# A retention layer and a quantized FFN on one core: the recurrence in halves of 64 tokens, one mask operation on VectorE, and an order written out call by call

## The reference

```python
q, k = rope(x @ Wq), rope(x @ Wk)          # 8 heads of 16 columns
v, g = x @ Wv, x @ Wg                      # 8 heads of 32 columns
s = log2(1.0 - exp2(-5.0 - arange(8)))
decay = where(diff >= 0, exp2(diff[None] * s[:, None, None]), 0.0)   # diff = query - key position
scores = einsum('bhqd,bhkd,hqk->bhqk', q * 16 ** -0.5, k, decay)
o = einsum('bhqk,bhkd->bhqd', scores, v)
o = o * rsqrt(mean(o * o, axis=-1) + EPS) * g_norm_w
x = layernorm(x + (o * (g * sigmoid(g))) @ Wo)
h = silu(fp4_linear(x, w_gate)) * fp4_linear(x, w_up)   # fp4_linear quantizes both operands
x = layernorm(x + fp4_linear(h, w_down))
```

## Time and profile before

| | us |
|---|---|
| median of 3 runs (137.73 to 137.95) | 137.76 |
| span of the profiled execution | 135.8 |
| PE busy | 121.6 (90%) |
| DVE busy | 112.9 (83%) |
| ACT busy | 98.0 (72%) |
| POOL busy | 96.6 (71%) |

### The profile page before, as it was taken

How to read it: one execution, slowest core, us unless ns; L and a number is a source line. 1 busy time by engine, 2 the same in 40 slices (tenths; PEclk the granted TensorE clock), 3 DMA queues, 4 the chain that set the end, 5 groups by cost and what they waited for, 6 DMA issues and landing times.

```text
span 135.8 us, 3550 instructions
## 1 busy us (share of the span) xinstructions
PE 121.6 (90%) x1248; PEld 79.6 (59%) x1248; DVE 112.9 (83%) x391; ACT 98.0 (72%) x311; POOL 96.6 (71%) x139
## 2 busy tenths in 40 slices
PE   4997998999999999999999999999999958888660
PEld 4755574755656566575758584848484745445450
DVE  1269889876879899999999999999999899999710
ACT  3055665778858787787888888888888978876753
POOL 4212856878677778878787979797979697656561
PEclk9999999999999999999999999999999999999999
DMA  3899980000000000000000000000000000000011
GB/s 105 262 250 237 409 288 5 7 2 0 5 0 0 5 0 2 0 7 0 0 5 0 0 7 19 0 19 7 19 0 24 0 19 19 22 19 19 27 54 59
DMA packets 6897, 6.53 MB, mean 48 GB/s; under 512 B 864, under 2 KB 6112, under 8 KB 6752
## 3 DMA queue, kind: packets, MB, share of 16 engines
q1 hardware_dynamic: 5856, 5.56, 13.6%
q10 hardware_dynamic: 1024, 0.76, 1.7%
HBM read 5.26 MB, written 1.05 MB: 46 GB/s over the span
## 4 chain that ended last, share of the span: by engine, by line
PE 75%; DVE 11%; ACT 8%; issue 3%; POOL 2%; POOLq 1%; DVEq 0%; ACTq 0%
PE ps L338 12%; PE ps L357 7%; PE ps L485 6%; PE ps L469 6%; PE ps L462 5%; PE ps L397 5%; PE ps L329 4%; PE ps L387 4%; PE ps L476 3%; PE ps L370 3%; PE ps L405 3%; PE ps L422 2%; PE ps L421 2%; PE ps L413 2%; PE ps L323 2%
## 5 line engine op out<-in xcount | busy, mean ns | idle before, releaser
L902 POOL TENSOR_TENSOR rstd_h<-ms,minus_half 128x8 f32<-128x8 f32 x16 | 26.4, 1647 | 7.7 <-DVE ms L767 7.0
L893 POOL TENSOR_TENSOR qk<-rope_c,rope_s 128x256 f32<-128x256 f32 x16 | 11.6, 726 | 13.0 <-DVE rope_s L744 12.9
L338 PE MATMUL ps<-w_vg,xT_sb 128*128 128x512 f32 x32 | 18.0, 645 | 0.0
L485 PE MATMUL ps<-wd_T,hT 128*128 128x128 f32 x96 | 13.6, 278 | 2.7 <-ACT hT L515 2.7
L927 POOL TENSOR_TENSOR hq<-h_grid,hs 128x352 f32<-128x352 f32 x16 | 13.0, 812 | 3.0 <-DVE h_grid L680 3.0
L516 ACT ACTIVATE q_eo<-ps,consts 128x128 f32<-128x128 f32 x32 | 11.8, 369 | 3.4 <-PE ps L347 3.4
L485 PEld LDWEIGHTS ps<-wd_T,hT 128*128 128x128 f32 x96 | 12.1, 193 | 3.5 <-DVE r L794 2.6
L740 DVE TENSOR_TENSOR rope_c<-ps,tabs_sb 128x256 f32<-128x256 f32 x16 | 6.8, 425 | 8.8 <-PE ps L329 8.8
L515 ACT ACTIVATE raw<-ps 128x512 f32<-128x512 f32 x16 | 9.6, 599 | 5.9 <-PE ps L357 5.9
L897 POOL TENSOR_SCALAR_AFFINE_SELECT probs<-raw 128x512 f32<-128x512 f32 x16 | 10.3, 642 | 4.7 <-ACT raw L515 4.6
L469 PE MATMUL ps<-wgu_T,xqT 128*128 128x352 f32 x32 | 12.4, 469 | 0.2
(11 more groups left out here) (112 smaller groups left out, 363.1 us busy)
## 6 DMA issues: line engine op xcount, KB each, us to landing
tabs_sb<-rope_tables SPq DMA_DIRECT2D x1, 1024.0 KB, 10.8
out<-x SPq DMA_DIRECT2D x16, 64.0 KB, 1.5
tabs_sb<-rope_tables SPq DMA_DIRECT2D x1, 640.0 KB, 7.3
xT_sb<-x_transposed SPq DMA_DIRECT2D x1, 512.0 KB, 8.7
x_res<-x SPq DMA_DIRECT2D x1, 512.0 KB, 11.4
xT_sb<-x_transposed SPq DMA_DIRECT2D x1, 320.0 KB, 6.2
x_res<-x SPq DMA_DIRECT2D x1, 320.0 KB, 7.9
w_vg<-in_w_vg ACTq DMA_DIRECT2D x1, 256.0 KB, 3.4
```

Source lines behind the costliest of these rows:

```text
L338: mm(vg_ps, xT(c), w_vg[:], start=True, stop=True).then_inc(vg_pe, 1)
L485: last = mm(down_ps, hT[:, c % 2, t, :], wd_T[:, t, :], start=t == 0, stop=t == 2)
L893: gp.tensor_tensor(qk[:, c % D, :], rope_c[:, c % D, :], rope_s[:, c % D, :], ALU.add).then_inc(qk_p, 1)
L902: gp.tensor_tensor(rstd_h[:, c, :], ms[:, c, :], minus_half[:], ALU.pow).then_inc(rms_p, 1)
```

## The change

Six things change, all in one step.

1. The recurrence runs in halves of 64 tokens. `C` stays 128 for everything else; `CH` is 64, and the decay tables are made for it. Scores are computed inside a half only: eight matmuls of 32 rows x 64 columns of the array over 128 columns, in the place of four over 256. `state_product`, `from_state` and `values` get twice as many matmuls with half the columns or half the rows each. The state is advanced twice a chunk, by two `next_state` calls (31 in all where there were 15).
2. The scores of all heads are now 128 x 512 numbers, and one DVE operation masks them from PSUM. The ACT copy to `raw` and the POOL mask are gone.
3. The stage loop is gone. Each engine's calls are written out one by one, and the three parts of the rotation, v's copy and the gate's silu are calls of their own.
4. Rings have 4, 6 or 8 slots; plus and grid of the quantization are written in place.
5. PSUM banks: scores and oT take banks 0 to 3 as a whole, o bank 0, xqT 1, yT 2; qk, qkT and down 4; vg, att and gate 5; hT 6; up 7; the state product 6 and 7.
6. Of the five `warm_up(4)` calls three are left, all ahead of the first state product.

```diff
+CH = C // 2
-    i = (np.arange(T) % C)[:, None]
-    dec = np.stack([np.exp((i + C) * lg) * DQK ** -0.5, np.exp(-i * lg)], 1)
+    i = (np.arange(T) % CH)[:, None]
+    dec = np.stack([np.exp((i + CH) * lg) * DQK ** -0.5, np.exp(-i * lg)], 1)
...
-        D = 3
-        q_eo = sb("q_eo", 128, D, 2, C)
-        probs = sb("probs", 128, 2, NH, C)
-        raw = sb("raw", 128, 2, NH - 2 * MB, C)
-        S = sb("S", 128, 2, 2 * DV)
+        q_eo = sb("q_eo", 128, D, 2, 2, CH)
+        probs = sb("probs", 128, D, NH, CH)
+        S = sb("S", 128, 8, 2 * DV)
...
+        BANKS = {"sc": (0, 1, 2, 3), "oT": (0, 1, 2, 3), "o": (0,), "yT": (2,), "qk": (4,), "qkT": (4,),
+                 "vg": (5,), "att": (5,), "xqT": (1,), "gate": (5,), "hT": (6,), "up": (7,),
+                 "down": (4,), "U": (6, 7)}
...
+            def occupy(name, banks):
+                for n in banks:
+                    free(n)
+                    tile[n] = name
                 filled[name] += 1
...
             def scores(c):
-                pe.wait_ge(qkT_act, 3 * (c + 1))
-                for j in range(NP):
-                    free_scores_bank(j)
-                    rows = slice(32 * j, 32 * j + 32)
-                    last = mm(sc_ps(j), kT[rows, c % D, :], q_eo[rows, c % D, :, :].rearrange("p e q -> p (e q)"),
-                              start=True, stop=True)
+                occupy("sc", BANKS["sc"])
+                for a in range(2):
+                    for j in range(NP):
+                        rows = slice(32 * j, 32 * j + 32)
+                        last = mm(sc_ps(j)[CH * a:CH * a + CH, :], kT[rows, c % D, CH * a:CH * a + CH],
+                                  q_eo[rows, c % D, a, :, :].rearrange("p e q -> p (e q)"), start=True, stop=True)
...
+            def state_product(c):
+                for j in range(NP):
+                    for a in range(2):
+                        keys = slice(CH * a, CH * a + CH)
+                        last = mm(U_ps(a)[32 * j:32 * j + 32, :], qk[keys, c % D, 128 + 32 * j:160 + 32 * j],
+                                  v_sb[keys, c % D, 64 * j:64 * j + 64], start=True, stop=True)
...
+            def from_state(c):
+                pe.wait_ge(state_v, 2 * c + 1)
+                occupy("oT", BANKS["oT"])
+                for a in range(2):
+                    for n in range(NH):
+                        j, e, slot32 = n // 2, n % 2, n % 4
+                        rows = slice(32 * j, 32 * j + 32)
+                        mm(oT_bank(n // 4, a)[32 * slot32:32 * slot32 + 32, :],
+                           S[rows, (2 * c + a) % 8, e * DV:(e + 1) * DV], q_eo[rows, c % D, a, e, :], start=True, stop=False)
...
-            for s in range(FIRST, LAST):
-                run = stage_runner(s)
-                run(state_product, 0)
-                run(values, 0)
...
+            warm_up(4); project_qk(0); warm_up(4); project_vg(0); transpose_qk(0); warm_up(4); state_product(0)
+            project_vg(1); scores(0); project_qk(1); project_vg(2); from_state(0); project_qk(2); values(0)
...
-            def copy_scores(c):
-                act.wait_ge(sc_pe, c + 1)
-                copy(raw[:, c % 2, :, :].rearrange("p (j e) q -> p j (e q)", e=2), ps[:, MB:4, 0:256]).then_inc(
-                    raw_act, 1)
...
             def mask_scores(c):
-                dve.wait_ge(c_ident, 2)
+                dve.wait_ge(c_ident, 3)
                 dve.wait_ge(sc_pe, c + 1)
-                vec.tensor_tensor(probs[:, c % 2, 0:2 * MB, :].rearrange("p (j e) q -> p j e q", e=2),
-                                  ps[:, 0:MB, 0:256].rearrange("p j (e q) -> p j e q", e=2),
-                                  causal[:].unsqueeze(1).unsqueeze(1).to_broadcast([128, MB, 2, C]),
+                vec.tensor_tensor(probs[:, c % D, :, :].rearrange("p (j e) q -> p j e q", e=2),
+                                  all_sc_ps.rearrange("p j (e q) -> p j e q", e=2),
+                                  causal[:].unsqueeze(1).unsqueeze(1).to_broadcast([128, NP, 2, CH]),
                                   ALU.mult).then_inc(mask_v, 1)
-            def next_state(c):
+            def next_state(c, a):
+                s = 2 * c + a
...
+                vec.scalar_tensor_tensor(S[:, (s + 1) % 8, :], S[:, s % 8, :], decay, U_ps(a), ALU.mult, ALU.add).then_inc(
                     state_v, 1)
```

More of the change, by code:

```diff
@@ L448, in transpose_down_weights @@
-                last.then_inc(wT_pe, 1)
-                fill(6, "weights")
+                    last = mm(wd_T_ps[:, t * C:(t + 1) * C], wd_q[:, t * C:(t + 1) * C], centring[:], start=True, stop=True)
+                last.then_inc(wd_pe, 1)
             def transpose_xq(c):
-                free_gate_bank()
                 pe.wait_ge(xq_p, c + 1)
-                transpose(xqT_ps, xq[:, c % 2, :], ident[:]).then_inc(xqT_pe, 1)
-                fill(6, "xqT")
+                occupy("xqT", BANKS["xqT"])
```

663 lines of the change are left out of this document (332 added, 331 removed).

## The result

The changed kernel takes 140.39 us (median of 4 runs, 139.76 to 143.77), the kernel before on the same chip 137.85: ratio 1.0168, 95% interval 1.0144 to 1.0191. It is slower by 1.7%. The forecast was 133.0 in a range of 128.8 to 139.5, with 0.18 for slower. The prediction was wrong.

A forecast was written before the change was run, and what follows sets the result against it. PE was taken to set the pace in full stages, DVE right behind. DVE's sum (128.6 plus 2.4 idle) and PE's (128.7 plus 2.4 waits) gave spans of 131.0 and 131.1; with 2.0 outside the span, 133.0 us, range 128.8 to 139.5.

The forecast's parts named there:

- The halves on PE: Tiled matmuls on PE: scores, from_state, state product and values fall from 1.72 to 1.35 us a chunk.
- the rule on overhead: Skill's rule on PE: about 60 cycles per matmul, so 48 more records would cost 1.2 us a chunk.
- the rival of a price for each record: PE's tiled matmuls cost the same per record whatever their columns, 1.44 us more a chunk: 151.7 us, chance 0.06.
- The handoffs: PE waiting at banks for DVE's mask and the oT copy; 2.4 us taken for either engine's lost time.
- s: PE's waits at new handoffs from chunk 3 to 15: 1.4 us if on time, 6.4 if late, 2.4 taken.
- The rival of PE stalling at the banks: DVE and ACT 0.55 us late at each of two handoffs, s about 10.5: 141.2 us, chance 0.12.
- the late gating: One late gating on DVE holds all scores on PE, since four banks must be free at once.
- DVE's busy time: DVE's sum: 10.2 us of idle filled, 3.2 added, last h_grid ends at 122.0; busy 116 us.
- The state steps: 16 more state steps on DVE, 0.20 us each: 3.2 us, up to 4.5.
- DVE takes over: Rival: DVE bounds full stages at 6.64 us, order wins no idle time: 136.9 us, chance 0.10.
- neither engine sets the pace: ACT copy (9.6 us) and POOL mask (10.3 us) go, which gives no time by itself.
- `values` of chunk 3 at 28.6: On PE, chunk 3's values stay at 28.6 us, because DVE must still quantize all weights by then.

The follow-up runs named there:

- e5: Changed kernel with GpSimd's four wide operations keeping two inputs but narrowed to 8 to 22 columns, other products left out: 132.74 us, ratio 0.9623.
- e10: Kernel before the change with the same four GpSimd operations narrowed to 8 to 22 columns: 137.46 us, ratio 0.9975.
- e4: Changed kernel with the two state steps of chunk 0 moved behind the weights' row maximum and mask_scores(0) on DVE: 140.89 us, ratio 1.0207.
- e9: Changed kernel with GpSimd's four wide operations reading one tensor, narrowed to last as long as in the changed kernel: 135.36 us, ratio 0.9809.
- e13: Changed kernel, whole, with nine swaps in DVE's list where two-input operations were held up by wide GpSimd ones: 139.97 us, ratio 1.0152.
- e1: Changed kernel with GpSimd's four wide operations reading one tensor times 1.0 instead of two: 139.25 us, ratio 1.0084.
- e14: Changed kernel, whole, with scores(0) ahead of project_vg(0) on PE and the ScalarE and DVE lists to match: 145.02 us, ratio 1.0501.

## Why the prediction was wrong

The range missed the time by 0.9 us, the forecast by 7.4, and it had the wrong sign. By its own steps:

**The halves on PE: right.** Scores, from_state and values take 1.20 us together in chunk 7, forecast 1.21 (scores 0.08 more, the other two less). Neither the rule on overhead nor the rival of a price for each record holds.

**The handoffs: right on DVE, too small on PE.** DVE is idle for 110 - 107.2 = 2.8 us between 12 and 122 (under 3 forecast). PE's weight loads wait 2.2 us for the mask in 5 places, 2.7 for gated in 6 and 1.6 for the copy of oT in 6: 6.5 us where s was put at 2.4. The rival of PE stalling at the banks had the right sign and, with 141.2 us, nearly the time, and named the late gating. But these waits don't make the difference: e5, which has the forecast's time, has 1.9, 3.0 and 1.4, that is 6.3.

**DVE's busy time: the step that failed.** "DVE: up to the last h_grid's end at 129.0 it is idle for 10.7 - 2.1 (the DMA, which stays) + 1.6 = 10.2 us that a better order could fill" and "+ 3.2". This sum takes over all 391 DVE instructions at the durations of the trace before, and these held only in that order. e4 against the forecast: busy 121.4 for 116, idle 139.3 - 121.4 = 17.9 for 131.0 - 116 = 15.0, together 8.3 us of span. In the busy part two errors are of opposite sign. The state steps, which I put at 3.2, made 1.2 (e5 against e10). The hold-ups, which I did not put at all, made 8.4 in e4, where the trace before had 1.2 of them. So 8.4 - 1.2 too little and 3.2 - 1.2 too much leave 5.2 of the 5.4. Of the 8.3 us of span 5.7 go with the hold-ups in e9 (span 133.6), and in e5 another 2.6 with POOL's length (131.0). That e5 lands on the forecast is in part luck: with 2 us less of state steps than I counted, and hold-ups of before gone that I had kept, it should have come out below it, and did not, since its idle time is larger than forecast.

**The rivals.** The nearest is "DVE takes over": DVE is the bound, as it said, but at a price that it did not know of (it gave 136.9).

**POOL: the part I left out.** I wrote of ACT and POOL that "neither engine sets the pace, so this gives no time by itself", looked at what leaves POOL, and not at what its remaining wide operations run beside. The trace of before had signs of it. In seven stages from 60 us on x_ratio takes 0.40 us beside hq, where x_plus and x_grid of the same shape take 0.29, and one operation of the weights takes 1.43 us beside qk, where the two others of its shape take 0.88:

```profile
73.26 0.79 POOL L927 TENSOR_TENSOR hq<-h_grid,hs 128x352 f32<-128x352 f32 x1
73.80 0.40 DVE L671 SCALAR_TENSOR_TENSOR x_ratio<-x_blocks,xs 128x128 f32<-128x128 f32 x1
```

I did not ask why. The control e10 shows that little there depended on it (0.4 us): it became dear when the order changed.

**The start and the end.** I left `values` of chunk 3 at 28.6 on the ground of the weights alone; it came at 31.18 (28.39 before, read the same way), that of chunk 15 at 107.43 (100.6). So 2.6 us were lost ahead of chunk 3, 4.2 between the two, and in e4 1.5 behind (139.3 - 107.4 = 31.9 for 131.0 - 100.6 = 30.4). The hold-ups are in all three (mask_scores(4) 1.2 us earlier in e9, 0.3 of it there from mask_scores(0) on, the stretch behind it 2.8 shorter, the end 1.7). Of the 2.6 us ahead of chunk 3 another 0.6 is TensorE's slower pace in this trace: in e13, with the same lists up to there, `values` of chunk 3 comes at 30.54. What is left, about 1 us, no run explains.

What stays open: how much the start costs by its order, and whether any order of the whole kernel avoids the meetings without idle time. That the hold-ups cost 5 us is shown only with work left out; the one whole kernel with fewer of them, e13, gained 0.4. It comes nearest to the kernel before in the new order, with 139.97, and none beats it.

## What to carry to other kernels

A duration read from a trace holds for what runs beside it: before an order is rewritten, list for each VectorE operation with two SBUF inputs which wide GpSimd operation it will meet, since on a full VectorE most of it comes back in the time (here 6.7 us of busy time and 5.0 of time, e9). A fixed stage loop can hide such a cost by chance, and a control on the kernel before (here a gain of 0.4 against 7.7 us) tells whether the operation or the order is to blame. Where every engine runs a list in order, a swap of neighbours can take a stall away and bring it back as idle time (here 4.5 us of hold-ups for 0.4 of time, e13): count the idle time beside the busy time before it is called a gain.

## What was unexpected of the hardware

- A VectorE operation with two SBUF inputs that starts while a wide GpSimd operation with two inputs runs waits until that is nearly through: 0.52 to 1.10 us beside hq or qk, 0.29 to 0.88 beside hq, 0.29 to 0.63 beside y. Beside GpSimd operations with one input, as wide, it is held less and seldom: nine times by 0.13 to 0.27 us in e1, twice by 0.15 and 0.17 in e9, else by 0.1 at most. Beside pow on 1 or 8 columns with two inputs it is not held.
- The other way round GpSimd waits: in the kernel before, hq took 1.00 us at 123.66, behind an h_ratio that had started at 123.49, where 0.79 is usual.
- One operation with one SBUF input was held too: a maximum over 128x44 of the weights took 0.50 us beside qk in the changed kernel (12.87), and 0.17 in e5.
- On GpSimd a product of 352 columns with a constant (one input) took 1103 ns, with a second tensor 813.
- A state step on VectorE (128 x 64, one input from PSUM) lasts 266 to 281 ns and holds it for 0.20, but 16 of them more made only 1.2 us of busy time (e5 against e10).
- In e14, 3 us in which TensorE was busy for 0.66 were followed by 6 us at a granted clock of 0.5.
